# A second tile for the projection weights, and the K0d_t load moved ahead of the transposes: an attention and FFN layer on eight cores

## The reference, cut to what matters

```python
xn = layernorm(x)                       # x: 4 x 8192 x 1024, the layer works on 4096 rows per core
k = fft(xn @ Wk.T + bk); v = fft(xn @ Wv.T + bv); q = fft(xn @ Wq.T + bq)
queried = cumsum(k * v, axis=1) * conj(q)
queried = queried / (1e-9 + norm(queried, axis=-1))
attn = real(ifft(queried)) / sqrt(1024)

h = concatenate([xn, -xn], axis=-1)
h = relu(s0 * h @ sign(k0)) * 2         # 2048 -> 4096, sign(b) is +1 or -1
h = relu(s1 * h @ sign(k1)) * 2         # 4096 -> 4096
ffn = s2 * h @ sign(k2)                 # 4096 -> 1024
out = x + attn + ffn
```

## Time and profile before

| what | us |
|---|---|
| runs shown | 3983.16 and 4114.90, median 4049.03 |
| the profiled execution | 3982.78 |
| its span, slowest core (core 6) | 3981.1 |
| spans of the other cores | 3965.3 to 3980.8 |
| TensorE busy in the span | 3643.8 (92%) |

### The profile page before, as it was taken

One profiled execution on the slowest core, in us unless ns is written; L12 is line 12 of the kernel. 1 busy time (PEld: TensorE's weight loads), 2 busy tenths in 40 slices (PEclk: granted clock), 3 DMA queues, 4 the chain that ended last, 5 costly groups with the idle time before them and its releaser, 6 DMA issues.

```text
span 3981.1 us, 43754 instructions; the slowest of 8 cores (3965.3 to 3981.1 us)
## 1 busy us (share of the span) xinstructions
PE 3643.8 (92%) x16512; PEld 1590.0 (40%) x16512; DVE 1120.6 (28%) x1586; ACT 1130.6 (28%) x1504; POOL 729.4 (18%) x907
## 2 busy tenths in 40 slices
PE   4658889989984999999999999999999999999998
PEld 1323333333332444444444444444444444444443
DVE  0034447867850112011211211111121111112112
ACT  3744443554562110311311121031112103112110
POOL 0023225545530001001100200110020010011001
PEclk8778889999997999999999999999999999999999
DMA  4143337345215333433343434343343433334343
GB/s 85 22 102 89 85 87 118 78 97 87 66 41 169 138 148 124 151 148 136 132 156 148 161 115 152 136 135 149 148 159 117 155 130 127 151 138 146 127 157 129
DMA packets 329182, 491.53 MB, mean 123 GB/s; under 512 B 217360, under 2 KB 219408, under 8 KB 295184
## 3 DMA queue, kind: packets, MB, share of 16 engines
q0 software_dynamic: 105072, 402.70, 30.5%
q1 hardware_dynamic: 218896, 66.12, 7.8%
q10 hardware_dynamic: 5008, 19.93, 1.3%
HBM read 276.87 MB, written 58.72 MB: 84 GB/s over the span
## 4 chain that ended last, share of the span: by engine, by line
PE 84%; DMA 4%; DVE 3%; issue 3%; ACT 3%; SPq 2%; POOL 0%; ACTq 0%; DVEq 0%; POOLq 0%
PE pd L977 44%; PE pd L661 13%; PE pd L1033 11%; PE pd L933 10%; PE pd L666 2%; PE pd L297 2%; SPq L533 1%; DMA xn_f<-xn_dram 1%; DMA wtmp<-Wk 1%; PE pd L504 1%; DMA K0d_t<-k0s 1%; DVE xn_t L482 1%; DVE bx_t L1069 1%; DMA xn_dram<-xn_t 1%; DVE bx_t L1061 1%
## 5 line engine op out<-in xcount | busy, mean ns | idle before, releaser
L977 PE MATMUL pd<-r_t,w1r 128*128 128x512 bf16 x8192 | 1769.4, 379 | 7.8 <-ACT r_t L947 7.8
L977 PEld LDWEIGHTS pd<-r_t,w1r 128*128 128x128 bf16 x8192 | 801.0, 98 | 976.2 <-issue 11.5
L995 DVE TENSOR_SCALAR w1r<-w1r 128x4096 bf16<-128x4096 bf16 x232 | 284.7, 1227 | 1637.3 <-DMA w1r<-w1s 1637.3
L933 PE MATMUL pd<-xn_f,K0d_t 128*128 128x512 bf16 x2048 | 456.9, 386 | 96.9 <-DMA K0d_t<-k0s 60.5
L1003 ACT ACTIVATE r_t<-pd,s_scales 128x512 bf16<-128x512 f32 x256 | 176.0, 687 | 1113.1 <-PE pd L977 1112.3
L990 POOL DMA_DIRECT2D w1r<-w1s x232 | 124.9, 538 | 1878.2 <-PE pd L977 1765.8
L1033 PE MATMUL pd<-w2ring,r_t 128*128 128x512 bf16 x2048 | 443.4, 379 | 7.8 <-ACT r_t L1003 7.8
L933 PEld LDWEIGHTS pd<-xn_f,K0d_t 128*128 128x128 bf16 x2048 | 202.5, 99 | 351.2 <-issue 120.4
L1033 PEld LDWEIGHTS pd<-w2ring,r_t 128*128 128x128 bf16 x2048 | 199.6, 98 | 251.6 <-issue 12.6
L947 ACT ACT_TABLE_LOAD x64 | 82.1, 1283 | 577.2 <-DVE bx_t L1069 459.9
L1049 DVE TENSOR_SCALAR w2ring<-w2ring 128x1024 bf16<-128x1024 bf16 x224 | 95.7, 427 | 422.1 <-DMA w2ring<-k2u 422.1
(11 more groups left out here) (153 smaller groups left out, 2495.8 us busy)
## 6 DMA issues: line engine op xcount, KB each, us to landing
w1r<-w1s POOLq DMA_DIRECT2D x256, 1024.0 KB, 4.6
w2ring<-k2u POOLq DMA_DIRECT2D x256, 256.0 KB, 2.6
conv_t<-k0u POOLq DMA_DIRECT2D x64, 256.0 KB, 4.1
w1s<-k1u SPq DMA_DIRECT2D x32, 512.0 KB, 5.9
bx_t<-x_own POOLq DMA_DIRECT2D x32, 512.0 KB, 6.5
out<-bx_t ACTq DMA_DIRECT2D x32, 512.0 KB, 4.6
x_t<-x_extra POOLq DMA_DIRECT2D x8, 1024.0 KB, 9.1
k0s<-conv_o SPq DMA_DIRECT2D x32, 256.0 KB, 3.0
```

The lines of the kernel that those rows point to most:

```text
L933: inst = te.matmul(reg.ap, K0d_t[:, dk * F0 + m * 128: dk * F0 + (m + 1) * 128], xn_f[fb][:, dk * TST:(dk + 1) * TST], start=(dk == 0), st ...
L977: inst = te.matmul(reg.ap, w1ring[c % 3][:, k * 128:(k + 1) * 128], r0_t[:, k * TST:(k + 1) * TST], start=(k == 0), stop=(k == NF0 - 1))
L995: lambda: v.tensor_scalar(w1ring[c % 3][:], w1ring[c % 3][:], 2.0, -1.0, op0=OP.mult, op1=OP.add))
```

## The change

The first part gives the preamble two weight tiles, wtmp0 and wtmp1, used in turn, with a semaphore for each (s_wld and s_wldb). The second part moves the barrier and the three K0d_t loads ahead of the first two `emit_prep_b`, and so takes their 16 transposes out of `end_marks`; these transposes are now emitted by the loop over tiles.

```diff
+    s_wldb = Ctr("s_wldb")
...
-    wtmp = mk_sb(es_a0, "wtmp", [128, NDK * D], BF16)
+    wtmp2 = [mk_sb(es_a0, f"wtmp{i}", [128, NDK * D], BF16) for i in range(2)]
...
-    for p in ("k", "v", "q"):
+    for pi, p in enumerate(("k", "v", "q")):
+        wb = pi % 2
+        wtmp = wtmp2[wb]
+        wkey = f"wtmp{wb}"
+        wsem = s_wld if wb == 0 else s_wldb
...
-            dstep(g, "pool", s_wld, [], ["wtmp"],
+            dstep(g, "pool", wsem, [], [wkey],
                   lambda: g.dma_start(wtmp[:], Wmat[p].ap().rearrange("(k p) d -> p k d", p=128)))
...
-                    dep_wait(te, "pe", ["wtmp", trig_key], [])
+                    dep_wait(te, "pe", [wkey, trig_key], [])
...
+    end_marks = [(s_pe, s_pe.n), (s_act, s_act.n), (s_dve, s_dve.n),
+                 (s_pool, s_pool.n),
+                 (s_xnw, s_xnw.n), (s_xnw2, s_xnw2.n), (s_wld, s_wld.n),
+                 (s_wldb, s_wldb.n), (s_bld, s_bld.n)]
+    end_marks += [(c, c.n) for c in s_x + s_cv + s_xnt + s_pw + s_cw]
...
-    b_fk = {0: emit_prep_b(0), 1: emit_prep_b(1)}
-
-    end_marks = [(s_pe, s_pe.n), (s_act, s_act.n), (s_dve, s_dve.n),
...
+    b_fk = {}
     for j in range(NST + 1):
-        if 2 <= j < NST:
+        if j < NST:
             b_fk[j] = emit_prep_b(j)
         if j >= 1:
             emit_compute_b(j - 1, b_fk[j - 1])
```

More of the change, by code:

```diff
@@ L279, in _ @@
         step(v, "dve", s_dve, [], ["ones1"], lambda: v.memset(ones1_t[:], 1.0))
-    for p in ("k", "v", "q"):
+    for pi, p in enumerate(("k", "v", "q")):
[3 more added lines that the diff above has]
+        wsem = s_wld if wb == 0 else s_wldb
         @block.gpsimd
-        def _(g, p=p):
-            dstep(g, "pool", s_wld, [], ["wtmp"],
+        def _(g, p=p, wtmp=wtmp, wkey=wkey, wsem=wsem):
+            dstep(g, "pool", wsem, [], [wkey],
                   lambda: g.dma_start(wtmp[:], Wmat[p].ap().rearrange("(k p) d -> p k d", p=128)))
@@ L292, in _ @@
                 @block.tensor
-                def _(te, p=p, dm=dm, reg=reg, trig_t=trig_t, trig_key=trig_key):
-                    dep_wait(te, "pe", ["wtmp", trig_key], [])
+                def _(te, p=p, dm=dm, reg=reg, trig_t=trig_t, trig_key=trig_key,
+                      wtmp=wtmp, wkey=wkey):
+                    dep_wait(te, "pe", [wkey, trig_key], [])
                     pacq(te, reg)
@@ L302, in _ @@
                     v = s_pe.inc(inst)
-                    record(s_pe, v, ["wtmp", trig_key], [])
+                    record(s_pe, v, [wkey, trig_key], [])
                 pe_done = s_pe.n
@@ L853, in build_nc @@
     bx_t = [mk_sb(es_b, f"bx_t{i}", [128, D], F32) for i in range(4)]
[L855 to L869, removed]
-    b_fk = {0: emit_prep_b(0), 1: emit_prep_b(1)}
     end_marks = [(s_pe, s_pe.n), (s_act, s_act.n), (s_dve, s_dve.n),
                  (s_pool, s_pool.n),
-                 (s_xnw, s_xnw.n), (s_xnw2, s_xnw2.n), (s_wld, s_wld.n), (s_bld, s_bld.n)]
+                 (s_xnw, s_xnw.n), (s_xnw2, s_xnw2.n), (s_wld, s_wld.n),
+                 (s_wldb, s_wldb.n), (s_bld, s_bld.n)]
     end_marks += [(c, c.n) for c in s_x + s_cv + s_xnt + s_pw + s_cw]
@@ L904, in _, with emit_prep_b @@
                   k0s.ap()[6 * 128:8 * 128, :].rearrange("(k p) m -> p k m", p=128)))
+    def emit_prep_b(j):
+        fb = j % 2
+        fkeys = [f"xnf{fb}_{dk}" for dk in range(NDK)]
+        @block.sync
+        def _(sync, j=j, fb=fb, fkeys=fkeys):
+            for dk in range(NDK):
+                dstep(sync, "sp", s_xnt[fb], ["xn_dram0"], [fkeys[dk]],
+                      lambda dk=dk: sync.dma_start(
+                          xn_f[fb][:, dk * TST:(dk + 1) * TST],
+                          xn_dram.ap()[j * TST:(j + 1) * TST, dk * 128:(dk + 1) * 128],
+                          transpose=True))
+            for fk in fkeys:
+                track[fk] = [(s_xnt[fb], s_xnt[fb].n), {}]
+        return fkeys
     def emit_compute_b(j, fkeys):
```

## The result

The changed kernel takes 0.9933 of the time before, 95% interval [0.9919, 0.9948]: 26.7 us less on a median of 3988.8 us (21 to 32 by the interval). 44.1 us less had been forecast. The median of all its runs is 3969.68 us, outside the range given.

What follows compares the result with a forecast made beforehand. TensorE was busy 84% of the span, leaving the preamble's weight waits, then paced by ScalarE, and the passage's K0d_t wait. Gains of 33.2 + 10.9 = 44.1 us took 3982.8 to 3938.7 us, range 3921 to 3960.

Steps and rivals of the forecast that it cites:

- Part one: Preamble: a second weight tile removes TensorE's waits for Wv and Wq, ScalarE then setting the pace; gain 33.2 us.
- Wk keeps its time: Preamble: Wv, issued right behind Wk on POOL's queue, does not delay Wk, which still ends TensorE's wait at 36.81 us.
- the rival in which the loads share: Preamble: Wk and Wv interleave, Wk lands up to 17.3 us later, gain there 15.9 us, time 3956; 10 in 100.
- Wk landing after 38 us: Preamble: a sign named beforehand that would show the prediction wrong.
- Part two: Passage to stage B: K0d_t issued 21.75 us earlier, ahead of the transposes, which are late next; gain 10.9 us.
- at half the engines eight transposes take 12.0 us: Passage: behind K0d_t, with POOL's queue still busy, the xn_f0 transposes need 12.0 us, so stage B starts at 1235.5.
- the slow end: Passage: eight transposes take 18.5 us, as beside an earlier x load; start at 1242.0, gain 4.4 us.
- the 47 us named as a sign of being wrong: Passage: a wait before stage B longer than 47 us from the K0d_t issue would show the prediction wrong.
- The order in SP's queue: Passage: SP's queue lands in order, so the transposes move only when its K0d_t piece is through, at 1223.2 us.
- 261 GB/s for transposes: Passage: the skill page's rate, putting eight transposes through in 4 us for a gain of 18.9 us; not adopted.
- The one in which the transposes take the place of the wait: Passage: transposes come as slowly as beside the x load, part two gains 4.4 us, time 3945; 14 in 100.
- the rival on the slower side: Preamble: TensorE's clock falls to 1.2 GHz while ScalarE sets the pace, costing 62 us, time 4001; 3 in 100.

Runs made afterwards that it cites:

- the kernel with early transposes: The changed kernel with the first tile's eight xn_f0 transposes issued before stage A's last tail instead of behind K0d_t; ratio 0.9881 to the kernel before.
- the last version: Changed kernel with xn_f0 transposes before stage A's last tail, every other weight-group copy and the 24 bias copies on VectorE; ratio 0.9767, median 3893 us.

## Why the prediction was wrong

*Part one held, a little oversized.* That the two waits go, that Wv lands in time behind Wk, that ScalarE paces the groups at 1.96 us and not TensorE at 1.75: all shown. 33.2 us were worked out and 30.3 came in the mean of the cores. Two terms account for most of it. The waits were taken from core 6, whose Wv and Wq took 17.3 and 16.5 us to land; the means over the eight cores are 16.2 and 16.1, 1.5 us less. And Wk landed 1.0 us later in the mean (33.5 us after its issue, before 32.5). "Wk keeps its time" was nearly right; the rival in which the loads share, 17 us, is out. The sign "Wk landing after 38 us" did appear, at 38.68 us on core 2, but on two cores of the kernel before TensorE also waited longer than that for Wk (39.06 and 39.77 us), so it was a poor sign.

*Part two failed, and at one step: "at half the engines eight transposes take 12.0 us".* The barrier lifted at the time forecast, K0d_t took 27 to 31 us on core 2 as forecast, and the transposes were late next as forecast. But they needed 22 us after K0d_t in the mean, not 12.0, and not the 18.5 that I had taken for the slow end: that row came from transposes beside one x load of 1 MB, while here some 6 MB of POOL's loads followed K0d_t. TensorE started 51.1 us after the K0d_t issue in the mean, beyond the 47 us named as a sign of being wrong. The runs show what stands in place of the half: one packet for each of POOL's packets, which was 11.6% of the engines in the 12 us shown above, so that beside these loads the transposes end last. With that, the prediction's own figures would have given nearly that time: 14 us of POOL's work left and 6.0 us of the transposes are 20 us. So would rows of before: with the third w1r tile in, all loads were through, and VectorE could convert it 45.7 us after the K0d_t issue (1262.09 against 1216.35, core 6):

```profile
1262.09 1.23 DVE L964 TENSOR_SCALAR w1r<-w1r 128x4096 bf16<-128x4096 bf16 x1 [1.24 <-DMA w1r<-w1s]
```

The transposes add their own 6.0 us of work to that. It makes 51.7 us, about what was measured, and no gain.

I had looked at POOL's loads as something that is issued earlier "with it" and costs nothing. That is the mistake behind the step: a load that nobody waits for can still push one that is waited for. The order in SP's queue, which I argued from s0r and sG, was true but beside the point, since without it the time was the same. The Trainium skill's 261 GB/s for transposes ("DMA: Bandwidth & Descriptors", Latency and other measured facts), set aside in the prediction, is further off still: an estimate by it gives 4 us for eight, and they took 22 here; in the quiet tail SP's issues alone took 10 us.

*The rest of the miss was not traced to the change.* The kernel before has a median of 3988.8 us, 6.0 above the profiled execution on which the sum stood. Stage A is 3.0 us longer in the mean of the profiled execution, with single cores up to 996.1 us (before 985.2). Over the nine profiles that are read on all cores its mean lies between 981.8 and 987.1 us, at 983.6 in the kernel with early transposes and 981.9 in the last version, both of which have part one. So part one alone doesn't decide it; why a core waits longer there in one execution was not settled.

*The rivals.* The one in which the transposes take the place of the wait was the nearest; it still left a gain of 4.4 us, and there was none. The clock stayed at 1.00 through ScalarE's pacing (it was 0.57 in the bias groups behind, from 131 to 171 us, as in the kernel before from 163 to 206 us), so the rival on the slower side fell, and with it, here, what the Trainium skill tells of short waits for PSUM banks ("TensorE: Matmul & The Clock Gate", A second HAM failure mode).

## What to carry to other kernels

When a load is moved ahead of another, list everything that becomes free to run with it, on every queue, and add up its work: the saturated DMA engines here did not favour what was waited for. Put what is waited for where the engines are idle (here ahead of the tail), and hold back what isn't needed yet. When a wait goes away, ask which engine finishes last in that stretch; taking ScalarE's table-reloading copies out of the preamble was worth 42 us of it, more than the whole change.

## What the runs showed of the hardware

DMA transposes beside plain loads lose far more than their share of work. 16 of them alone took 51% of the engines for 23.5 us, yet eight needed 47 to 53 us from the K0d_t issue beside K0d_t and POOL's loads, and 31 to 35 beside K0d_t alone. Neither their queue (K0d_t on ACT) nor smaller packets of the w1r loads changed that. The DMA engines gave the queues that had work one packet each in turn (960 and 961; 534, 527 and 534; 1827 and 1835), and a packet of a transpose carried 240 B where one of POOL's loads carried 4.8 KB. What packets of the loads as small as the transposes' own would do was not run.
